# Graph attention on one core: record columns three groups ahead, and a quad's sums in front of the logits' transposes

## The chip, the core and the metric

The kernel runs on one core of a Trainium2 chip. It uses TensorE (PE), VectorE (DVE), ScalarE (ACT), GpSimd (POOL) and SyncE (SP), which run side by side, each working through its own queue of instructions in order and waiting on semaphores for the others. The metric is the device time of one execution in microseconds; the table gives the median of three runs.

## What is computed

The reference has two layers; the change touches only the first, a graph attention over 120,000 edges of 8 types between 3,750 nodes, with 4 heads of 64. The edges are sorted by destination.

```python
feat_all = jnp.einsum('ni,rhid->rnhd', inputs, conv_weights)
feat_src_e = feat_all[edge_type, edge_src]
feat_dst_e = feat_all[edge_type, edge_dst]
el = jnp.sum(feat_src_e * attn_l[edge_type], axis=-1)
er = jnp.sum(feat_dst_e * attn_r[edge_type], axis=-1)
e = jax.nn.leaky_relu(el + er, negative_slope=LEAKY_SLOPE)
m = jax.ops.segment_max(e, edge_dst, num_segments=N_NODES)
ex = jnp.exp(e - m[edge_dst])
denom = jax.ops.segment_sum(ex, edge_dst, num_segments=N_NODES)
alpha = ex / denom[edge_dst]
h = jax.ops.segment_sum(alpha[..., None] * feat_src_e, edge_dst, num_segments=N_NODES)
```

The second layer is a mixture of 8 experts, top 2, over the nodes.

## The kernel before

Five stages run one after the other: nodes (the projected features of every node and type, written to DRAM as `feats`, 260 words a row: 256 features and 4 left logits), edges, routing, experts, combination. Only `edge_stage` changes.

**Tiling.** A unit is 128 edges, a block two units. A pair is a block with one tile of 128 destination nodes. 16 pairs (32 units) make a group; there are 32 groups, the last two smaller (10 and 8 pairs). Within a group, a quad is 4 units or 2 pairs, so a full group has 8 quads. `each_period` writes a body for each group; on PE, ACT, DVE and SP group 0 stands alone, groups 1 to 24 are four rounds of a loop over six groups, and the rest is written out.

**One period, for group g.**
- SP loads the records of group g+2 (`load_meta`, 16 loads into `meta`), once the rows of group g are done (`rows_ready`).
- DVE, `meta_rows`: records to `rows`, `cat` and `reset`. PE, `meta_rows`: three transposes of `rows` into `psS` (L801). DVE, `meta_columns`: `typeT`, `idxT`, `ndlT`, then `idx_ready` (L580 to L583). Before, both are for group g+2.
- POOL, `gather_features`: after `idx_ready` one indirect DMA for each unit, 32 in all, into `gath`, which has three buffers (`GBUFS`). The gathers of a quad wait until the sums of the same quad three groups before are done.
- ACT, `one_hot`: from `ndlT` the matrix `hot` of a unit, for group g+1. PE, `turn`: its transpose; ACT, `copy`: to `hotT`. PE, `right_logits` (L825): the right logits of the edges into `psE`. DVE, `pick_right` (L589, L591) at the end of the period: `er_e` of group g+1.
- DVE, `logits` (L597, L598): after the gathers of g landed (`gath_in`), left and right logits into `e_sb`, then `e_ready`. PE: one transpose of `e_sb` into `psS` (L856), `eT_ready`. DVE, `chunk_maxima` (L604 to L607). PE: L868. DVE, `chain_maxima` (L617 to L638), `shifts`; PE and ACT between them; ACT's exponentials end with `exp_ready`.
- DVE, `scale` (L667): a quad of `gath` times its weights. PE, `total` (L840): for each of its two pairs, two accumulating products `hot` x `gath` into one of three banks of `psP`; each product is two matmul rows in the trace, so a pair is four and a quad eight. DVE, `add` (L676): the pair into its tile of `acc`, then `sum_used`.

**What sets the order.** It is written out by hand. PE's period has eight slots; slot s does `turn` of quad s and `right_logits` of quad s-1 of group g+1, and `total` of a quad: of g-1, quad s+3, in slots 0 to 4, and of g, quad s-5, in slots 5 to 7. `total` of a pair waits until the pair three before it has been added, because of the three banks. DVE's adds of quads 2 to 7 of group g-1 and of quads 0 and 1 of group g stand between its other steps: the add of quad 2 (pairs 4 and 5) directly behind `logits`, the add of quad 3 directly behind `chunk_maxima`.

## Time and profile before

| | us |
|---|---|
| median of three runs (2530.4 to 2534.8) | 2532.44 |
| the profiled run, its own time | 2529.42 |
| span of the profiled run | 2527.6 |
| edge stage, from SP's first record load to DVE's first instruction of the next stage | 283.4 to 1694.6 |
| PE, DVE, ACT, POOL busy over the span | 1860.7, 1148.7, 819.7, 1078.7 |
| mean granted clock of PE, as a share of 2.4 GHz | 0.828 |

The page gives busy time by engine and by line. A timeline row gives start, duration, engine, line, operation and output<-inputs, and in brackets the idle time before it with what ended it; "issue" is idle time that ended with nothing that the profile shows. Rows merged by the profile have a count (x8). PE's clock is granted at one of two levels, 2.4 or 1.2 GHz, which shows in the durations of the same matmuls. L597 is line 597 of the kernel before.

### The profile page before, as it was taken

The page shows a single profiled execution, that of the slowest core. Times are in us where ns is not written, and L with a number is a line of the kernel's source. Part 1 is how long each engine was busy: PE and PEld are TensorE (multiplying, and loading weights), DVE is VectorE, ACT ScalarE, POOL GpSimd, SP SyncE. Part 2 cuts the span into 40 slices and gives each one's busy share as a digit, 9 for nine tenths or more (in the row PEclk, how much of TensorE's full clock was granted, in tenths as well). Part 3 has the DMA queues.
Part 4 walks back from the last instruction along what each step waited for, and adds up shares of the span by engine and source line. Part 5 has one row for each costly group of instructions (what it writes and reads, how often), then busy time and mean ns, then how long its engine had stood idle before and what let it go on. Part 6 is the DMA issues. An engine that isn't in the chain of part 4 may idle for free. (4 is left out here: it accounts for less than half of the span.)

```text
span 2527.6 us, 38608 instructions
## 1 busy us (share of the span) xinstructions
PE 1860.7 (74%) x9120; PEld 1578.4 (62%) x9121; DVE 1148.7 (45%) x2882; ACT 819.7 (32%) x2109; POOL 1078.7 (43%) x1151
## 2 busy tenths in 40 slices
PE   6799377777777777877777878754119999999920
PEld 6688366666566665666666666544118888888820
DVE  2132136666566666666666667668411111111122
ACT  1122154444435344444444444301003223222200
POOL 1000077777676767676677777500440000000046
PEclk9899758887888788888888888875559999999965
DMA  5633244444333433343344344210135655555533
GB/s 192 249 135 153 83 117 112 111 113 107 93 106 103 109 99 106 103 111 103 102 108 106 104 113 110 77 49 17 56 138 177 205 179 201 190 193 200 184 91 113
DMA packets 127778, 317.14 MB, mean 125 GB/s; under 512 B 27207, under 2 KB 78151, under 8 KB 114020
## 3 DMA queue, kind: packets, MB, share of 16 engines
q0 software_dynamic: 53568, 148.39, 21.8%
q1 hardware_dynamic: 74020, 166.61, 19.1%
q8 instruction: 71, 1.16, 0.2%
q14 instruction: 119, 0.97, 0.1%
HBM read 251.75 MB, written 63.14 MB: 125 GB/s over the span
## 5 line engine op out<-in xcount | busy, mean ns | idle before, releaser
L552 POOL DMA_INDIRECT gath<-feats,idxT x996 | 947.1, 951 | 683.8 <-DVE ndlT L583 339.3
L840 PE MATMUL psP<-gath,hot 128*128 128x260 f32 x1992 | 627.6, 465 | 97.5 <-DVE acc L676 94.6
L840 PEld LDWEIGHTS psP<-gath,hot 128*128 128x128 f32 x1992 | 429.9, 229 | 194.3 <-DVE acc L676 108.6
L762 ACT ACTIVATE hot<-cst,ndlT 128x128 f32<-128x128 f32 x996 | 317.1, 392 | 46.7 <-DVE ndlT L583 31.5
L772 ACT COPY hotT<-psOT 128x512 f32<-128x512 f32 x249 | 144.3, 580 | 570.3 <-PE psOT L811 569.9
L667 DVE TENSOR_TENSOR gath<-gath,psA 128x1024 f32<-128x1024 f32 x249 | 301.2, 1220 | 18.0 <-ACT gath L789 11.3
L825 PEld LDWEIGHTS psE<-er,hotT 128*128 128x128 f32 x1992 | 280.7, 216 | 33.7 <-issue 31.4
L825 PE MATMUL psE<-er,hotT 128*128 x1992 | 278.5, 287 | 23.2 <-issue 23.2
L676 DVE TENSOR_TENSOR acc<-acc,psP 128x260 f32 x498 | 210.2, 422 | 116.7 <-PE psP L840 75.7
L1224 PE MATMUL psH<-xeT,w1buf 128*128 128x256 f32 x1184 | 262.8, 380 | 0.0
L1235 PE MATMUL psY<-w2buf,hT 128*128 128x256 f32 x1184 | 261.5, 379 | 0.0
L1224 PEld LDWEIGHTS psH<-xeT,w1buf 128*128 128x128 f32 x1184 | 226.0, 191 | 31.0
L401 PE MATMUL psF<-wext,xT 128*128 128x264 f32 x960 | 225.9, 394 | 23.5 <-ACT er L228 13.6
L1235 PEld LDWEIGHTS psY<-w2buf,hT 128*128 128x128 f32 x1184 | 222.2, 190 | 28.8
L1320 POOL COPY slot_col_c<-slot_i 128x2 int32 x30 | 5.8, 194 | 547.3 <-PEq L1313 546.3
L1279 DVE TENSOR_SCALAR xeT<-psX,w1buf 128x256 f32<-128x256 f32 x74 | 36.8, 539 | 412.9 <-DMA w1buf<-in_experts 400.0
L401 PEld LDWEIGHTS psF<-wext,xT 128*128 128x128 f32 x960 | 183.2, 194 | 57.1 <-ACT er L228 14.0
L1261 ACT ACTIVATE hT<-psH,w1buf 128x256 f32<-128x256 f32 x296 | 124.3, 471 | 264.3 <-PE psH L1224 264.1
L811 PE MATMUL psOT<-cst,hot 128*128 128x128 f32 x996 | 187.6, 320 | 8.3 <-issue 5.2
L811 PEld LDWEIGHTS psOT<-cst,hot 128*128 128x128 f32 x996 | 147.7, 172 | 46.1 <-issue 28.2
L765 ACT ACTIVATE hot<-hot 128x512 f32<-128x512 f32 x249 | 156.7, 629 | 7.9
L856 PE MATMUL psS<-cst,e_sb 128*128 128x128 f32 x32 | 15.2, 475 | 179.7 <-DVE e_sb L598 179.7
(190 smaller groups left out, 1220.3 us busy)
## 6 DMA issues: line engine op xcount, KB each, us to landing
w1buf<-in_experts SPq DMA_DIRECT2D x37, 1030.0 KB, 7.2
w2buf<-in_experts SPq DMA_DIRECT2D x37, 1024.0 KB, 5.4
feats<-frow SPq DMA_DIRECT2D x30, 1040.0 KB, 3.9
gath<-feats,idxT POOLq DMA_INDIRECT x996
slots_x<-acc SPq DMA_DIRECT2D x1, 9472.0 KB, 32.1
xrow<-slots_x SPq DMA_DIRECT2D x37, 256.0 KB, 6.5
slots_y<-yrow SPq DMA_DIRECT2D x37, 256.0 KB, 6.6
meta<-in_edges SPq DMA_DIRECT2D x512, 12.0 KB
```

The lines of the kernel that those rows point to most:

```text
L401: ins = pe.matmul(psF[:, n % BUFS, j, 0:W], xT[:, i % 2, k], wext[:, k, 2 * pair + j], start=k == 0, stop=k == KD - 1)
L552: pool.indirect_dma_start(gath[:, r, u], None, feats, bass.IndirectOffsetOnAxis(ap=idxT[:, q, u:u + 1], axis=0)).then_inc(gath_in[r], 16)
L667: dve.tensor_tensor(feat, feat, alpha.unsqueeze(3).to_broadcast([P, QUAD, HEADS, HD]), ALU.mult).then_inc(scaled, 1)
L676: dve.tensor_tensor(into[b % PQ], into[b % PQ], psP[:, b % BANKS, 0:FW], ALU.add).then_inc(sum_used, 1)
L762: ins = act.activation(hot[:, q, u], iota, ACT.Square, bias=ndlT[:, q, u:u + 1])
L765: act.activation(hot[:, q, j * QUAD:(j + 1) * QUAD], hot[:, q, j * QUAD:(j + 1) * QUAD], ACT.Relu, bias=1.0, scale=-1.0).then_inc(hot_read ...
L772: act.copy(hotT[:, j % 2], psOT[:]).then_inc(hotT_copied, 1)
L811: ins = pe.transpose(psOT[:, k * P:(k + 1) * P], hot[:, q, j * QUAD + k], ident)
L825: ins = pe.matmul(psE[:, u * W // 512, u * W % 512:u * W % 512 + W], hotT[:, j % 2, k * P:(k + 1) * P], tables[k // BLK], start=True, stop ...
L840: ins = pe.matmul(psP[:, b % BANKS, 0:FW], hot[:, q, u], gath[:, r, u], start=u % BLK == 0, stop=u % BLK == BLK - 1)
L1224: ins = pe.matmul(psH[:, bank(q, m // MG), (m % MG) * SLOT_TILE:(m % MG + 1) * SLOT_TILE], w1(q, k, m), xeT[:, q, k], start=k == 0, stop=k ...
L1235: ins = pe.matmul(psY[:, j, 0:D], hT[:, q, m, j * P:(j + 1) * P], w2(q, m), start=m == 0, stop=m == KH - 1)
```

## The change

Five tiles (`reset`, `cat`, `idxT`, `ndlT`, `typeT`) get three buffers, numbered by group modulo 3 like `gath`, where they had two. DVE's and PE's `meta_rows` and DVE's `meta_columns` in period g are for group g+3 in place of g+2, and three groups, not two, are done ahead of the loop. SP's loads and their waits are unchanged. In PE's period the transpose of `e_sb`, which stood in slot 0 between `turn` and `total`, stands behind slot 0. The changed kernel is two lines shorter from there on.

```diff
-        reset = t("reset", [P, 2, UNIT + 1])
-        cat = t("cat", [P, 2, 5])
-        idxT = t("idxT", [P, 2, GU], I32)
-        ndlT = t("ndlT", [P, 2, GU])
-        typeT = t("typeT", [P, 2, GU, RELS])
+        reset = t("reset", [P, GBUFS, UNIT + 1])
+        cat = t("cat", [P, GBUFS, 5])
+        idxT = t("idxT", [P, GBUFS, GU], I32)
+        ndlT = t("ndlT", [P, GBUFS, GU])
+        typeT = t("typeT", [P, GBUFS, GU, RELS])
...
-                meta_rows(0, 0)
-                meta_columns(0, 0)
-                meta_rows(1, 1)
-                meta_columns(1, 1)
+                for g in range(GBUFS):
+                    meta_rows(g, g % 2, g)
+                    meta_columns(g, g)
                 pick_right(0, 0)
...
-                    if there(g + 2):
-                        meta_rows(g + 2, q)
+                    if there(g + 3):
+                        meta_rows(g + 3, 1 - q, r)
...
-                    if there(g + 2):
-                        meta_columns(g + 2, q)
+                    if there(g + 3):
+                        meta_columns(g + 3, r)
...
-                meta_rows(0)
-                meta_rows(1)
+                for g in range(GBUFS):
+                    meta_rows(g)
                 for j in range(SLOTS_Q):
                     turn(0, 0, j)
                     right_logits(0, j - 1)
...
                 def period(g, q, r, n):
                     def slot(s):
                         turn(g + 1, 1 - q, s)
-                        if s == 0:
-                            pe.wait_ge(e_ready, g + 1)
-                            pe.transpose(psS[:, S_ET:S_ET + P], e_sb[:, 1], ident).then_inc(eT_ready, 1)
                         right_logits(g + 1, s - 1)
-                        if s == 5 and there(g + 2):
-                            meta_rows(g + 2)
+                        if s == 5 and there(g + 3):
+                            meta_rows(g + 3)
...
                     slot(0)
+                    pe.wait_ge(e_ready, g + 1)
+                    pe.transpose(psS[:, S_ET:S_ET + P], e_sb[:, 1], ident).then_inc(eT_ready, 1)
                     slot(1)
```

PE, slot 0 of a period in the loop, before; the names in brackets are the semaphores that the instruction waits for:

```order
L811 MATMUL psOT<-cst,hot 128x128 [waits hotT_copied,hot_ready]
L811 MATMUL psOT<-cst,hot 128x128 x3
L856 MATMUL psS<-cst,e_sb 128x128 [waits e_ready]
L833 REGISTER_ALU
L836 REGISTER_ALU [waits scaled]
L840 MATMUL psP<-gath,hot 128x260 [waits sum_used]
L840 MATMUL psP<-gath,hot 128x260
L836 REGISTER_ALU
L840 MATMUL psP<-gath,hot 128x260 [waits sum_used]
L840 MATMUL psP<-gath,hot 128x260
L807 REGISTER_ALU
```

The same place after:

```order
L810 MATMUL psOT<-cst,hot 128x128 [waits hotT_copied,hot_ready]
L810 MATMUL psOT<-cst,hot 128x128 x3
L832 REGISTER_ALU
L835 REGISTER_ALU [waits scaled]
L839 MATMUL psP<-gath,hot 128x260 [waits sum_used]
L839 MATMUL psP<-gath,hot 128x260
L835 REGISTER_ALU
L839 MATMUL psP<-gath,hot 128x260 [waits sum_used]
L839 MATMUL psP<-gath,hot 128x260
L863 MATMUL psS<-cst,e_sb 128x128 [waits e_ready]
L806 REGISTER_ALU
```

Both pairs' products, each with its wait for a bank, have moved in front of the wait for the logits.

DVE, ahead of the first period; what stands between the second group's columns and the first `pick_right`, before:

```order
L580 TENSOR_TENSOR typeT<-psS,cst 128x256 [waits rowsT_ready]
L582 CAST idxT<-psS 128x32 [waits v_step_edges]
L583 TENSOR_SCALAR ndlT<-psS 128x32
L589 TENSOR_TENSOR er_all<-psE,typeT 128x1024 [waits er_done]
L591 TENSOR_REDUCE er_e<-er_all 128x128 [waits v_step_edges]
```

After:

```order
L583 TENSOR_SCALAR ndlT<-psS 128x32
L565 SCALAR_TENSOR_TENSOR rows<-meta 128x128 [waits meta_in0]
L566 CAST rows<-meta 128x128
L567 TENSOR_SCALAR rows<-meta,tile_off 128x128
L570 TENSOR_SCALAR cat<-rows,tile_of 128x2 [waits rows_ready]
L572 COPY cat<-rows 128x1
L573 MEMSET reset 128x2
L574 TENSOR_TENSOR reset<-rows 128x127
L575 TENSOR_SCALAR reset<-reset 128x127 [waits v_step_edges]
L580 TENSOR_TENSOR typeT<-psS,cst 128x256 [waits rowsT_ready]
L582 CAST idxT<-psS 128x32 [waits v_step_edges]
L583 TENSOR_SCALAR ndlT<-psS 128x32
```

Eleven instructions of the third group, the first with a wait for its records, stand in front of `pick_right`. On PE the three transposes of its rows stand in front of the first `turn`.

## Rows read from the trace of the kernel before

**Rows 1.** Page, costliest groups (busy, mean ns | idle before); then L597 by source.

```profile
L552 POOL DMA_INDIRECT gath<-feats,idxT x996 | 947.1, 951 | 683.8 <-DVE ndlT L583 339.3
...
L597 DVE TENSOR_TENSOR e_sb<-gath,er_e x32: 291/292/344, 352.3 to 1666.2; 128x128 f32<-128x128 f32 x32
```

**Rows 2.** Waits over the span: us in total, times, longest.

```profile
POOL gath L552 <- DVE ndlT L583: 339.3, 16, 300.7
POOL gath L552 <- issue: 285.1, 933, 0.6
...
PE psS L856 <- DVE e_sb L598: 179.7, 32, 7.1
...
DVE lv L617 <- PE psS L868: 57.1, 32, 4.3
```

**Rows 3.** Timeline of PE, parts of two periods: start, us, engine, instructions.

```profile
1011.63 1.12 PE L811 MATMUL psOT<-cst,hot 128*128 128x128 f32 x4
1012.54 1.76 PE L825 MATMUL psE<-er,hotT 128*128 x8
...
1035.19 0.64 PE L811 MATMUL psOT<-cst,hot 128*128 128x128 f32 x4
1041.55 0.48 PE L856 MATMUL psS<-cst,e_sb 128*128 128x128 f32 x1 [5.72 <-DVE e_sb L598]
1041.82 3.67 PE L840 MATMUL psP<-gath,hot 128*128 128x260 f32 x8
1045.29 0.82 PE L811 MATMUL psOT<-cst,hot 128*128 128x128 f32 x4
1045.95 0.98 PE L825 MATMUL psE<-er,hotT 128*128 x8
1046.76 2.00 PE L840 MATMUL psP<-gath,hot 128*128 128x260 f32 x8
1048.69 0.43 PE L868 MATMUL psS<-spread,cst 128*4 128x160 f32 x2
```

**Rows 4.** Timeline of DVE, the same period and the next logits.

```profile
1040.72 0.29 DVE L597 TENSOR_TENSOR e_sb<-gath,er_e 128x128 f32<-128x128 f32 x1 [2.85 <-issue]
...
1041.41 0.98 DVE L676 TENSOR_TENSOR acc<-acc,psP 128x260 f32 x2
1042.43 1.22 DVE L667 TENSOR_TENSOR gath<-gath,psA 128x1024 f32<-128x1024 f32 x1
1043.57 0.41 DVE L604 TENSOR_TENSOR_SCAN seg<-reset,psS 128x128 f32<-128x128 f32 x1
...
1044.92 0.42 DVE L676 TENSOR_TENSOR acc<-acc,psP 128x260 f32 x1
...
1049.16 0.18 DVE L617 COPY lv<-psS 4x32 f32<-4x32 f32 x1 [1.84 <-PE psS L868]
...
1082.73 0.29 DVE L597 TENSOR_TENSOR e_sb<-gath,er_e 128x128 f32<-128x128 f32 x1 [2.86 <-issue]
```

**Rows 5.** Timeline of POOL: the first gather of each of two groups.

```profile
1028.45 0.95 POOL L552 DMA_INDIRECT gath<-feats,idxT  x1 [2.16 <-PE psP L840]
...
1072.15 0.95 POOL L552 DMA_INDIRECT gath<-feats,idxT  x1 [3.72 <-DVE ndlT L583]
```

**Rows 6.** Timelines of DVE and SP at the start of the edge stage.

```profile
304.76 0.29 DVE L565 SCALAR_TENSOR_TENSOR rows<-meta 128x128 f32<-128x128 int32 x1 [22.55 <-DMA meta<-in_edges]
...
326.22 0.29 DVE L565 SCALAR_TENSOR_TENSOR rows<-meta 128x128 f32<-128x128 int32 x1 [19.09 <-DMA meta<-in_edges]
...
389.95 0.29 DVE L597 TENSOR_TENSOR e_sb<-gath,er_e 128x128 f32<-128x128 f32 x1 [4.20 <-DMA gath<-feats,idxT]
...
283.41 106.21 SPq L530 DMA_DIRECT2D meta<-in_edges  x80
```

**Rows 7.** Timeline of DVE: a group's rows in a period, up to the next add.

```profile
1021.92 0.29 DVE L565 SCALAR_TENSOR_TENSOR rows<-meta 128x128 f32<-128x128 int32 x1 [1.69 <-issue]
...
1023.48 0.42 DVE L676 TENSOR_TENSOR acc<-acc,psP 128x260 f32 x1
```

More of the change, by code:

```diff
@@ L568, in meta_rows, with meta_columns, pick_right @@
                     dve.wait_ge(rows_ready, g + 1)
-                    dve.tensor_scalar(cat[:, q, 2:4], rows[:, 1, 0:UNIT:UNIT - 1], 64.0, sb["tile_of"][:, bass.ds(g, 1)],
+                    dve.tensor_scalar(cat[:, r, 2:4], rows[:, 1, 0:UNIT:UNIT - 1], 64.0, sb["tile_of"][:, bass.ds(g, 1)],
                                       ALU.mult, ALU.add)
-                    dve.tensor_copy(cat[:, q, 4:5], rows[:, 1, 0:1])
-                    dve.memset(reset[:, q, 0:UNIT + 1:UNIT], 0.0)
-                    step(dve.tensor_tensor(reset[:, q, 1:UNIT], rows[:, 1, 1:UNIT], rows[:, 1, 0:UNIT - 1], ALU.not_equal))
-                    dve.tensor_scalar(reset[:, q, 1:UNIT], reset[:, q, 1:UNIT], -BIG, None, ALU.mult)
-                def meta_columns(g, q):
+                    dve.tensor_copy(cat[:, r, 4:5], rows[:, 1, 0:1])
+                    dve.memset(reset[:, r, 0:UNIT + 1:UNIT], 0.0)
+                    step(dve.tensor_tensor(reset[:, r, 1:UNIT], rows[:, 1, 1:UNIT], rows[:, 1, 0:UNIT - 1], ALU.not_equal))
+                    dve.tensor_scalar(reset[:, r, 1:UNIT], reset[:, r, 1:UNIT], -BIG, None, ALU.mult)
+                def meta_columns(g, r):
                     dve.wait_ge(rowsT_ready, g + 1)
-                    step(dve.tensor_tensor(typeT[:, q], psS[:, 2 * P:3 * P:HEADS].unsqueeze(2).to_broadcast([P, GU, RELS]),
+                    step(dve.tensor_tensor(typeT[:, r], psS[:, 2 * P:3 * P:HEADS].unsqueeze(2).to_broadcast([P, GU, RELS]),
                                            iota8.unsqueeze(1).to_broadcast([P, GU, RELS]), ALU.is_equal))
-                    dve.tensor_copy(idxT[:, q], psS[:, 0:P:HEADS])
-                    dve.tensor_scalar(ndlT[:, q], psS[:, P:2 * P:HEADS], -1.0, None, ALU.mult).then_inc(idx_ready, 1)
-                def pick_right(g, q):
+                    dve.tensor_copy(idxT[:, r], psS[:, 0:P:HEADS])
+                    dve.tensor_scalar(ndlT[:, r], psS[:, P:2 * P:HEADS], -1.0, None, ALU.mult).then_inc(idx_ready, 1)
+                def pick_right(g, r):
                     dve.wait_ge(er_done, quads_before(g) + quads(g))
@@ L638, in chain_maxima, with shifts @@
                     step(dve.tensor_copy(r_last[:, 0:1], r_last[:, used:used + 1]))
-                def shifts(g, q):
-                    fwd, bwd = reset[:, q, 0:UNIT], reset[:, q, UNIT:0:-1]
+                def shifts(g, r):
+                    fwd, bwd = reset[:, r, 0:UNIT], reset[:, r, UNIT:0:-1]
                     dve.wait_ge(yzT_ready, g + 1)
@@ L706, in period @@
                     scale(before, rb, 4)
-                    chunk_maxima(g, q)
+                    chunk_maxima(g, r)
                     add(before, 3, sums3)
@@ L717, in period @@
                     sums5, sums6 = load_tiles(before, 5), load_tiles(before, 6)
-                    shifts(g, q)
+                    shifts(g, r)
                     add(before, 5, sums5)
@@ L740, in period @@
                     if there(g + 1):
-                        pick_right(g + 1, 1 - q)
+                        pick_right(g + 1, (r + 1) % GBUFS)
                     assert isinstance(g, int) or step.n == STEPS, step.n
@@ L751, in _, with one_hot @@
             def _(act):
-                def one_hot(g, q, j):
+                def one_hot(g, q, r, j):
                     if j >= quads(g):
@@ L761, in one_hot @@
                         u = j * QUAD + k
-                        ins = act.activation(hot[:, q, u], iota, ACT.Square, bias=ndlT[:, q, u:u + 1])
+                        ins = act.activation(hot[:, q, u], iota, ACT.Square, bias=ndlT[:, r, u:u + 1])
                     ins.then_inc(squared, 1)
@@ L772, in copy, with both @@
                     act.copy(hotT[:, j % 2], psOT[:]).then_inc(hotT_copied, 1)
-                def both(g, q, js):
+                def both(g, q, r, js):
                     for j in js:
-                        one_hot(g, q, j)
+                        one_hot(g, q, r, j)
                         if j:
                             copy(g, j - 1)
-                both(0, 0, range(SLOTS_Q))
+                both(0, 0, 0, range(SLOTS_Q))
                 copy(0, SLOTS_Q - 1)
                 def period(g, q, r, n):
-                    both(g + 1, 1 - q, range(5))
+                    both(g + 1, 1 - q, (r + 1) % GBUFS, range(5))
                     act.wait_ge(dnT_ready, g + 1)
@@ L790, in period @@
                                    ACT.Exp).then_inc(exp_ready, 1)
-                    both(g + 1, 1 - q, range(5, SLOTS_Q))
+                    both(g + 1, 1 - q, (r + 1) % GBUFS, range(5, SLOTS_Q))
                     copy(g + 1, SLOTS_Q - 1)
```

14 lines of the change are left out of this document (7 added, 7 removed).

## The prediction

> **What bounds the kernel now.** I began with the page's groups and the waits, then laid the time rows of PE and DVE in one period of the edge stage side by side, then read the start of that stage. The edge stage repeats one period per group of edges; the 32 logits instructions at L597 run from 352.3 to 1666.2 [rows 1], so a period takes 1313.9 / 31 = 42.4 us. No engine fills it. GpSimd comes closest: 996 gathers of 951 ns, with 285.1 us of issue time between them, are 1.24 us each, 39.6 us for the 32 of a full group, and it has idle time besides [rows 1, 2]. The period is a ring of hand-overs between PE and DVE. Its widest hole on PE is the wait for the logits, 179.7 us in 32 times, 5.6 us each. DVE in turn waits for PE's L868, 57.1 us in 32 times, 1.8 us each [rows 2]. So in the stretch from the logits to L617, PE's queue ends last and DVE has 1.8 us to spare.
>
> In one period: PE ends the one-hot transposes at 1035.83, is idle until 1041.55, transposes the logits, runs quad 3's eight matmuls (3.67 us), then transposes, right logits, quad 4's matmuls and L868 at 1048.69 [rows 3]. DVE makes the logits at 1040.72, adds pairs 4 and 5, scales quad 4, is ready for the logits' maxima at 1043.57 with no wait, adds pair 6 at 1044.92, and waits 1.84 us for L868 before L617 at 1049.16 [rows 4].
>
> **Part 1, quad 3's sums in front of the logits' transposes.** The quad is pairs 6 and 7, four matmuls each. psP has three banks: pair 6 needs pair 3 added, done in the previous period; pair 7 needs pair 4 added, and that add stands on DVE behind the logits. So only half the quad can move into the 5.7 us hole, and the other half now stands between the logits and their transposes.
>
> Pair 6 starts at 1035.8 at the fast rate, half of quad 4's 2.00 us = 1.0, and is out of the way by 1036.9. Pair 7 starts after pair 4's add, which is half of the 0.98 us from 1041.41, so at 1041.95, and takes half of 3.67 us = 1.84: until 1043.8. The transpose (0.48) then ends near 1044.3. Two consequences:
> - DVE's maxima start 1044.3 instead of 1043.57, 0.7 us later. That fits into the 1.84 us that DVE waits for L868 today: 1.1 us of it are left [rows 4].
> - PE begins slot 1 near 1044.05 instead of 1045.29, 1.24 us earlier. Not all of this arrives. The matmuls after the hole run at half rate until about 1045.9: eight in 3.67 us against 2.00 [rows 3]. If this stretch ends at the same time as before, slot 1 now lies in it: its transposes cost up to 1.12 instead of 0.82, and part of its right logits goes at 1.76 instead of 0.98, together 0.3 to 0.6 lost. Pair 9 needs pair 6's add, now ending at 1046.0; PE reaches pair 9 near 1047, so that doesn't bind.
>
> So L868 and L617 come 0.6 us earlier. After L617 all is a chain (some twenty small DVE steps, then PE waiting for DVE's adds), which only shifts. Bounds: 0.2 if slot 1 is slow throughout (1.24 - 0.30 - 0.78), and 1.1, the DVE wait that is left. I take **0.6**, the reading in the middle of the slow stretch. The 31 periods with a quad in front give 31 x 0.6 = **-18.6 us** (-6 to -34).
>
> **Part 2, columns three groups ahead.** In the loop this moves no work off PE or DVE: the same eleven DVE instructions and three transposes stand in the same slots, for group g+3. It releases GpSimd: of its waits for L583, 339.3 - 300.7 = 38.6 us, those inside the loop, go [rows 2]. Nobody waits for that. Gathers of the group that starts at 1028.45 end before 1072.15 minus the 3.72 us wait, at 1068.4, and their logits come at 1082.73, 14 us later [rows 4, 5]. So **0 us** in the loop. If this cover were gone, the price would be what the gathers are late; none shows. SP's loads keep their wait (rows of g done, group g+2 loaded), which now comes a period sooner, and the loads stay two periods ahead of use.
>
> It costs something at the start. Before the first one-hot transpose PE now also has to pass the third group's rows transposes, and those wait for its records. SP issues record loads back to back, 80 in 106.21 us, 1.33 each, 21.2 us for a group's 16; the first group's landed for DVE at 304.76, the second's at 326.22 [rows 6], so the third's at 347.5. DVE, PE (its turns, its right logits), ACT's copies behind PE's turns and then pick_right and the logits all come 21.3 us later. What comes back is small: the second logits had waited 4.20 us for gathers, where 2.86 us is the usual gap [rows 4, 6]; with everything later the gathers are there, so 1.3 us return. **+20.0 us**, bounds 18 and 21.5. Nothing hides it: the period that follows has no slack of that size on any engine, since the ring has none.
>
> One period at the end has no rows and columns any more. Up to the next add they take DVE from 1021.92 to 1023.48, 1.56 us [rows 7], on DVE's path between two adds: **-1.5 us** (0 to -2.5).
>
> **Sum.** +20.0 - 18.6 - 1.5 = -0.1 us. The profiled run took 2529.42 us, so 2529.3; the median of the runs shown is 3.0 us above it. The forecast is **2532 us**, no measurable change, where 0.2% or 5 us is about what a measurement can tell. By the bounds: best 18 - 34 - 2.5 = -18.5, worst 21.5 - 6 = +15.5.
>
> **Rivals.**
> - *The slow stretch swallows the gain* (2542 us). PE comes back from the hole at half rate, and with its matmuls earlier more of slot 1 is slow. For: eight matmuls take 3.67 us after the hole in this period, and right logits elsewhere take 1.76. Against: the slow stretch has to reach past 1046. At 0.2 to 0.3 us per period it gives -8, so +20 - 8 - 1.5 = +10.5. This is the case that ends slower, and it decides from a gain under 0.45 us per period, where the net is above +5.
> - *DVE's chain becomes the bound* (2572 us). If the maxima come so late that L617 no longer waits for PE, each period grows by about 0.7 instead of shrinking: 31 x 0.7 + 18.5 = +40. It needs the transposed logits more than 1.8 us late; worked out they are 0.7. Unlikely.
> - *PE's clock stays up* (2517 us). Four matmuls cut the hole from 5.7 to about 5.1 us, and the return after it may then be at the fast rate. Pair 7 takes 1.0, the transposed logits are there for DVE near 1043.5 with no delay, and L617 can come 1.1 us earlier: 31 x 1.1 = 34, net 20 - 34 - 1.5 = -15.5. Against it: 5.1 us is still nearly the whole hole. The Trainium skill, "TensorE: Matmul & The Clock Gate", Part 1, says of the clock: "the default state is throttled, and activity releases the throttle". By that rule filling the hole is right in kind; the slow 3.67 us after it agree with the rule, and whether four matmuls suffice no row of before shows.
> - *The gathers did bind* (2464 us). If some of GpSimd's lateness is hidden in the 2.86 us before each logits, the period could fall to GpSimd's own 39.6: 31 x 2.8 = 87, net 20 - 87 - 1.5 = -68. The 14 us of margin speak against it.
> - *The third group's records cost nothing* (2512 us), if the added DVE and PE work did not stand in the queues in front of the first turns; the order of instructions says that it does.
>
> **How the numbers follow.** Forecast 0.41 (gain 0.45 to 0.8 per period, own range 2526 to 2538); slow stretch 0.22; clock up 0.22; DVE bound 0.07; gathers 0.04; free start 0.04. Range: 2510 to 2550. It takes in the forecast, the slow stretch and the clock case with the bounds of the sum around 2532 (+15.5 gives 2548, -18.5 gives 2514) and a little beyond, and leaves out DVE bound, gathers and the edges of the rest, under 0.2. Faster by over 0.2%: clock 0.22, gathers 0.04, free start 0.04 and 0.07 of the forecast, 0.37. Slower: 0.22 + 0.07 and 0.03 of the forecast, 0.32. The rest, 0.31, is no change.
>
> **What the new profile would show.** The first logits near 373.8 instead of 352.3, the second near 410 without a wait for gathers; a third wait of DVE for records, about 19 us. In the loop: four psP matmuls right behind the one-hot transposes, then an idle time of about 5 us that ends with DVE's add (L676) and not with the logits; L604 waiting some 0.7 us for PE; L617's wait down from 1.8 to about 0.5; 41.8 us per period; GpSimd's waits for ndlT gone. Wrong would be: first logits before 365, a period above 42.4, eight matmuls behind the transposes instead of four in front, or L617 not waiting at all.

## The result and the profile after

| | before | after |
|---|---|---|
| median of four runs each, on the same chip, us | 2532.28 | 2583.15 |
| lowest and highest, us | 2530.4 to 2534.8 | 2582.65 to 2585.49 |
| profiled run, us (span) | 2529.42 (2527.6) | 2585.49 (2583.7) |
| mean granted clock of PE | 0.828 | 0.814 |
| first, second, last logits, us | 352.3, 389.95, 1666.15 | 371.40, 407.30, 1721.19 |

After/before is **1.021, 95% interval 1.0196 to 1.0224**: 50.9 us slower. The forecast was 2532 us, no measurable change, with a range up to 2550. The time lies 33 us above that range.

The difference of the two profiled runs, 56.1 us, splits at the logits (L597): +17.4 up to the second ones, +37.7 in the 30 periods from there to the last (1313.9 us against 1276.2, which is 1.26 a period), +0.3 to the end of the edge stage, +0.8 behind it. So the start cost about what was forecast, and the loop, which should have given 18.6 us, took 37.7.

The page after: its first lines, and the two groups that answer to [rows 1] and to the quads' sums.

```profile
span 2583.7 us, 38612 instructions
...
PE 1917.8 (74%) x9120; PEld 1618.0 (63%) x9121; DVE 1153.9 (45%) x2882; ACT 819.2 (32%) x2109; POOL 1079.0 (42%) x1151
...
L552 POOL DMA_INDIRECT gath<-feats,idxT x996 | 947.7, 952 | 698.0 <-DVE ndlT L583 316.6
...
L839 PE MATMUL psP<-gath,hot 128*128 128x260 f32 x1992 | 662.0, 483 | 249.7 <-DVE acc L676 246.7
```

The same 9120 matmuls keep PE busy for 1917.8 us where it was 1860.7: 57.1 us more for the same work, while PE's idle time stays what it was (2583.7 - 1917.8 = 665.9 us against 666.9). DVE, ACT and POOL are busy as before. That is the first sign of where the time went: not a new wait, but slower matmuls.

The waits of after (us in total, times, longest), beside [rows 2]:

```profile
POOL gath L552 <- DVE ndlT L583: 316.6, 19, 298.5
...
PE psP L839 <- DVE acc L676: 246.7, 87, 6.6
...
POOL gath L552 <- PE psP L839: 110.6, 94, 4.4
...
DVE lv L617 <- PE psS L866: 22.2, 32, 3.1
```

PE's wait for the logits, 179.7 us before, is gone; in its place stands the wait for DVE's add. DVE's wait at L617 fell from 57.1 to 22.2 us, as the change means it to. GpSimd waits more for free buffers (94 times, 110.6 us) and less for indices: besides the longest wait, 316.6 - 298.5 = 18.1 us are left of the 38.6 that the prediction expected to go.

PE in one period of after, which answers to [rows 3] (start, us, engine, line, work, idle before):

```profile
1074.35 1.04 PE L839 MATMUL psP<-gath,hot 128*128 128x260 f32 x4
1080.81 2.10 PE L839 MATMUL psP<-gath,hot 128*128 128x260 f32 x4 [5.42 <-DVE acc L676]
1082.71 0.42 PE L863 MATMUL psS<-cst,e_sb 128*128 128x128 f32 x1
1082.92 1.06 PE L810 MATMUL psOT<-cst,hot 128*128 128x128 f32 x4
1083.77 1.14 PE L824 MATMUL psE<-er,hotT 128*128 x8
1084.74 2.00 PE L839 MATMUL psP<-gath,hot 128*128 128x260 f32 x8
...
1091.70 2.10 PE L839 MATMUL psP<-gath,hot 128*128 128x260 f32 x4 [2.23 <-DVE acc L676]
...
1094.77 1.11 PE L810 MATMUL psOT<-cst,hot 128*128 128x128 f32 x4
1095.68 1.75 PE L824 MATMUL psE<-er,hotT 128*128 x8
1097.25 3.81 PE L839 MATMUL psP<-gath,hot 128*128 128x260 f32 x8
1100.85 0.42 PE L875 MATMUL psS<-cst,dn 128*128 128x128 f32 x1
```

And PE of before in the second half of that stretch, which the rows ahead of the prediction did not reach:

```profile
1053.76 1.14 PE L840 MATMUL psP<-gath,hot 128*128 128x260 f32 x4 [2.27 <-DVE acc L676]
...
1055.42 0.66 PE L811 MATMUL psOT<-cst,hot 128*128 128x128 f32 x4
1055.91 0.98 PE L825 MATMUL psE<-er,hotT 128*128 x8
1056.72 1.12 PE L840 MATMUL psP<-gath,hot 128*128 128x260 f32 x4
1059.46 2.10 PE L840 MATMUL psP<-gath,hot 128*128 128x260 f32 x4 [1.61 <-DVE acc L676]
1061.36 0.42 PE L877 MATMUL psS<-cst,dn 128*128 128x128 f32 x1
```

Read them as pairs. The hole ahead of the period's first sums is 5.42 us against 5.72, and the matmuls behind it are at the lower rate in both (four in 2.10 us after, eight in 3.67 before). The second hole has the same length, 2.23 against 2.27 us, and ends with the same add. Before, the four matmuls behind it take 1.14 us; after, they take 2.10, and everything behind them up to L875 is slow too: one-hot transposes 1.11 against 0.66, right logits 1.75 against 0.98, eight sums 3.81. From the first of these sums to the `dn` transpose it is 9.15 us after and 7.60 before.

The two periods stand for the rest in the main point. Over the 22 periods from the third logits to the 25th, the four matmuls behind the second hole (pair 11) take 1.14 to 1.15 us in every period of before and 2.10 in every period of after, behind holes of 2.38 and 2.48 us on average. Beyond that pair the rows of before show a better period than most: the next one (pair 12), 1.12 us here, takes over 1.6 us in 15 of the 22 periods of before and in all 22 of after.

The loop's windows (us, then busy time with instructions of PE, PEld, DVE, ACT and POOL, then PE's granted clock, DMA share, GB/s), from the third to the 25th logits; before, then after:

```profile
433.10:1385.76 952.66, 729.99 (x3762) 604.50 (x3762) 618.34 (x1562) 424.89 (x1122) 675.62 (x712) 0.83 0.40 105
```

```profile
451.30:1437.99 986.69, 779.25 (x3762) 641.20 (x3762) 623.13 (x1563) 424.59 (x1122) 691.02 (x726) 0.80 0.39 104
```

With the two levels at 1 and 0.5 of full speed, a mean clock c means a share 2 x (1 - c) at the lower one: 0.34 of 43.3 us before, 0.40 of 44.9 after. Summed from the clock's records it is 15.1 us a period before and 18.3 after. For the same 3762 matmuls PE is busy (779.25 - 729.99) / 22 = 2.24 us longer in each period.

The full period of before is 43.3 us, and not the prediction's 42.4: that is a mean over all 31 periods, with the shorter ones at the end in it.

Means over those 22 periods, in us after L597's start, show where in the period the time is won and lost:

| | before | after | difference |
|---|---|---|---|
| DVE's maxima start (L604) | 2.73 | 3.35 | +0.62 |
| DVE L617 | 8.27 | 7.52 | -0.75 |
| DVE L649 (end of the small steps) | 18.11 | 17.40 | -0.71 |
| PE's `dn` transpose (L877, after L875) | 20.74 | 21.47 | +0.73 |
| DVE's rows (L565) | 24.87 | 25.58 | +0.70 |
| DVE `pick_right` (L589) | 37.41 | 38.94 | +1.53 |
| next logits | 43.30 | 44.85 | +1.55 |

The gain is there, of the size forecast, and it holds as far as L649. Then 1.4 us are lost around the second hole and another 0.8 in the last slots, where slow stretches stand as well. The gain of 0.75 and the 1.55 that the period is longer make 2.30, about the 2.24 by which PE's busy time grew. One slow stretch of the last slots:

```profile
1107.91 3.68 PE L839 MATMUL psP<-gath,hot 128*128 128x260 f32 x8 [0.56 <-DVE acc L676]
```

Before, the same eight took 1.99 us, at 1068.38.

**Theory.** The moved matmuls change how PE's work and idle time lie in the period, and more of the work then runs at the lower clock; the hand-overs themselves are right. **Rivals.** (a) The three-deep columns cost the time, through GpSimd or the DMAs. (b) The logits' transpose now waits behind pair 7, and that delay costs it. (c) The gathers collide with the sums that now start earlier.

### The profile page after: what moved, and what is told of

Same layout as the page of the kernel before. It is cut to its first block and busy times, and to the rows that moved or that the text cites. A ratio compares the mean times of both kernels' runs of the same rounds, so it can differ in the third digit from the quotient of the medians.

```text
span 2583.7 us, 38612 instructions
## 1 busy us (share of the span) xinstructions
PE 1917.8 (74%) x9120; PEld 1618.0 (63%) x9121; DVE 1153.9 (45%) x2882; ACT 819.2 (32%) x2109; POOL 1079.0 (42%) x1151
## 5 line engine op out<-in xcount | busy, mean ns | idle before, releaser
L552 POOL DMA_INDIRECT gath<-feats,idxT x996 | 947.7, 952 | 698.0 <-DVE ndlT L583 316.6
L839 PE MATMUL psP<-gath,hot 128*128 128x260 f32 x1992 | 662.0, 483 | 249.7 <-DVE acc L676 246.7
L839 PEld LDWEIGHTS psP<-gath,hot 128*128 128x128 f32 x1992 | 439.5, 235 | 354.2 <-DVE acc L676 264.2
L824 PEld LDWEIGHTS psE<-er,hotT 128*128 128x128 f32 x1992 | 294.0, 225 | 38.8 <-issue 36.5
L824 PE MATMUL psE<-er,hotT 128*128 x1992 | 290.1, 294 | 28.2 <-issue 28.2
L667 DVE TENSOR_TENSOR gath<-gath,psA 128x1024 f32<-128x1024 f32 x249 | 301.2, 1219 | 17.0 <-ACT gath L788 10.3
L810 PE MATMUL psOT<-cst,hot 128*128 128x128 f32 x996 | 195.2, 330 | 7.3 <-ACT hot L764 6.0
L1094 POOL DMA_INDIRECT slots_x<-xn,slot_col x60 | 57.6, 959 | 219.1 <-DVE xn L1078 199.3
```

What stands on the lines that cost most here:

```text
L552: pool.indirect_dma_start(gath[:, r, u], None, feats, bass.IndirectOffsetOnAxis(ap=idxT[:, r, u:u + 1], axis=0)).then_inc(gath_in[r], 16)
L667: dve.tensor_tensor(feat, feat, alpha.unsqueeze(3).to_broadcast([P, QUAD, HEADS, HD]), ALU.mult).then_inc(scaled, 1)
L810: ins = pe.transpose(psOT[:, k * P:(k + 1) * P], hot[:, q, j * QUAD + k], ident)
L824: ins = pe.matmul(psE[:, u * W // 512, u * W % 512:u * W % 512 + W], hotT[:, j % 2, k * P:(k + 1) * P], tables[k // BLK], start=True, stop ...
L839: ins = pe.matmul(psP[:, b % BANKS, 0:FW], hot[:, q, u], gath[:, r, u], start=u % BLK == 0, stop=u % BLK == BLK - 1)
```

## Experiments

### On a chip of another kind

The first runs fell on chips on which the kernel before itself takes 3600 to 3700 us. In what follows, the first kind of chip is the one on which it takes about 2530 us.

**e1_order_alone**: `before` with PE's order changed and nothing else.

```diff
-                        if s == 0:
-                            pe.wait_ge(e_ready, g + 1)
-                            pe.transpose(psS[:, S_ET:S_ET + P], e_sb[:, 1], ident).then_inc(eT_ready, 1)
...
                     slot(0)
+                    pe.wait_ge(e_ready, g + 1)
+                    pe.transpose(psS[:, S_ET:S_ET + P], e_sb[:, 1], ident).then_inc(eT_ready, 1)
```

> The kernel before with the logits' transposes behind quad 3's sums and nothing else changed. Both theories (the clock theory: PE spends more of each period at its lower clock; the order theory: a wait of PE or DVE grew) expect the loss in the loop here: 30 periods x 1.3 us = 38 us, so about 2568 us, a period near 43.8 us, the first logits at 352. If the columns made three groups in advance had a share in the loop's loss, this run is well below 2568.

**e2_ahead_alone**: `after` with the transpose put back into slot 0, so only the columns are three groups ahead (the same lines the other way round).

> The kernel after with the logits' transposes back in slot 0, between the one-hot transposes and quad 3's sums: columns three groups ahead alone. Expected by both: the start only, +17 us (in the changed kernel the second logits came 17.4 us later), no change in the loop, 1 us less at the end: about 2549 us. A rival, that the earlier gathers disturb the loop, expects a period above 42.5 us and more than 2555 us.

**e3_between_pairs**: `before` with the transpose between pair 6 and pair 7, so that it need not wait for pair 7.

```diff
+                        if between and b == PQ * j:
+                            between()
...
+                    def between():
+                        pe.wait_ge(e_ready, g + 1)
+                        pe.transpose(psS[:, S_ET:S_ET + P], e_sb[:, 1], ident).then_inc(eT_ready, 1)
```

> The kernel before with pair 6 (the first half of quad 3) in front of the logits' transposes and pair 7 behind them. DVE's maxima then wait for nothing new. Order theory (PE's wait for the add of pair 4 in front of the logits' transposes costs the time): the loss is gone and L617 comes over 1 us earlier than before: 2500 to 2515 us. Clock theory (taking work out of the time behind the hole lets the lower clock reach further into the period): L617 comes earlier too, but the matmuls of pair 11 and of slots 2 and 3 run at the lower rate, and the total is 2530 to 2570 us.

**e4_order_filled**: e1, with the hole between pair 6 and pair 7 filled by eight matmuls whose result nobody reads (every group but the first).

```diff
+                    def between():
+                        for _ in range(0 if isinstance(g, int) and g == 0 else 8):
+                            pe.matmul(psS[:, 0:2 * P], ident, cst[:, 0:2 * P], start=True, stop=True)
```

> The order of e1 with 8 extra 128x256 matmuls (some 3.6 us at the higher clock) in the hole between pair 6 and pair 7, written into a part of psS that nobody needs at that time; they compute nothing that is used. Clock theory: the stretch at the lower clock behind the hole goes or gets shorter, and the period falls well below e1's 43.8, to 41 to 42 us: 2490 to 2520 us in spite of the extra work. Order theory: the period stays at 43.8 or above: 2565 us or more.

**e5_before_filled**: `before` with ten such matmuls in front of the wait for the logits.

```diff
                         if s == 0:
+                            for _ in range(0 if isinstance(g, int) and g == 0 else 10):
+                                pe.matmul(psS[:, 0:2 * P], ident, cst[:, 0:2 * P], start=True, stop=True)
                             pe.wait_ge(e_ready, g + 1)
```

> The kernel before with 10 extra 128x256 matmuls (some 4.4 us at the higher clock) in the hole of 5.7 us between the one-hot transposes and the logits' transposes, written into a part of psS that nobody needs at that time; they compute nothing that is used. Clock theory: the eight matmuls of quad 3 behind the logits' transposes take 2.0 us, not 3.7, the period gets shorter by 1 us or more, 2485 to 2510 us. If the lower clock costs nothing on the ring of waits, 2532 us or slower by what the filler delays.

**e6_after_again**: the changed kernel as it is, to see what kind of chip this is.

> The changed kernel itself, once more, beside the kernel before. In the earlier runs of this study the kernel before took 3612 to 3686 us instead of 2532, with 40 us in every period in which DVE (L589) and ACT (L772) wait while GpSimd works through a group's gathers. If that state holds here too, the changed kernel, whose gathers start earlier, takes about 2950 us like the run with the columns three groups ahead alone; if it doesn't, 2583 us.

| | us | before on that chip | ratio, 95% interval |
|---|---|---|---|
| e1_order_alone | 3703.01 | 3686.29 | 1.0042 (1.0023 to 1.0061) |
| e2_ahead_alone | 2938.55 | 3686.29 | 0.7973 (0.7929 to 0.8017) |
| e3_between_pairs | 3707.29 | 3686.29 | 1.0062 (1.0041 to 1.0083) |
| e4_order_filled | 3706.96 | 3686.29 | 1.0058 (1.0034 to 1.0082) |
| e5_before_filled | 3622.36 | 3612.11 | 1.0014 (0.9980 to 1.0048) |
| e6_after_again | 2985.05 (one run) | 3703.32 | 0.81 |

None of e1 to e5 came near its expected time, and these runs answer another question than the one asked; e6 took 2985 us, where 2950 was expected if the chip was of this kind. The waits of e1:

```profile
PE psP L840 <- DVE acc L676: 1252.5, 89, 45.2
ACT hotT L772 <- remote: 1114.9, 41, 39.3
DVE er_all L589 <- remote: 1083.8, 28, 41.8
```

and one period of it, from the timelines of POOL, PE, DVE and ACT ("remote": the profile shows nothing that released the wait):

```profile
1508.72 0.94 POOL L552 DMA_INDIRECT gath<-feats,idxT  x1 [45.55 <-PE psP L840]
...
1547.46 0.95 POOL L552 DMA_INDIRECT gath<-feats,idxT  x1 [0.30 <-issue]
```

```profile
1516.65 1.07 PE L825 MATMUL psE<-er,hotT 128*128 x8 [1.90 <-issue]
...
1560.32 2.10 PE L840 MATMUL psP<-gath,hot 128*128 128x260 f32 x4 [39.67 <-DVE acc L676]
```

```profile
1553.97 1.23 DVE L589 TENSOR_TENSOR er_all<-psE,typeT 128x1024 f32<-128x1024 f32 x1 [40.48 <-remote]
```

```profile
1554.03 0.58 ACT L772 COPY hotT<-psOT 128x512 f32<-128x512 f32 x1 [33.85 <-remote]
```

DVE waits for right logits whose matmuls PE has on record at 1516.65, and goes on only at 1553.97, after the last of the 32 gathers of the group. Then PE starts, then GpSimd: the gathers and the rest of the period stand one behind the other, 82 us in place of 43. The gathers themselves take 0.95 us each as elsewhere. With the columns three groups ahead, GpSimd has its indices early and its gathers overlap more of the period (in e2 DVE's wait is no longer among the largest, ACT's is 404.4 us where e1 has 1114.9), and the kernel takes 0.80 of the time.

The filler of e4 shows more. Its sixteen rows wait for nothing, and while the gathers run PE still starts them one at a time:

```profile
1529.09 0.59 PE L858 MATMUL psS<-cst 128*128 128x256 f32 x1 [2.27 <-issue]
1531.90 0.59 PE L858 MATMUL psS<-cst 128*128 128x256 f32 x1 [2.21 <-issue]
```

From one row's start to the next it is 2.1 us in the median there, and 0.22 in f4, the same kernel on a chip of the first kind. So on these chips PE too falls behind during the gathers, in instructions that no semaphore holds, and the long waits of DVE and ACT need not be waits for a semaphore alone. What slows them is not shown by any record, and stays open.

It also means that the fillers of e4 and e5 don't keep PE busy here, and the matmuls behind the first hole stay slow (pair 7 of e5 takes 1.83 us on average). The second hole differs as well: e1's pair 11 takes over 1.6 us in 7 of 22 periods, where f1 below has 22 of 22. e1, e3 and e4 differ by less than their intervals. So the theory had to be tested without the gathers, or on a chip like the first.

### Without the gathers

The n-kernels leave out the gathers of groups 3 to 31 and the waits for them; the buffers keep the first groups' rows, so their times stand for the ring of PE, DVE and ACT alone. This time the chip was of the first kind, `before` at 2530.66 us.

```diff
-                each_period(pool, gather_features, GBUFS, GROUPS - 3)
+                for g in range(GBUFS):
+                    gather_features(g, g % 2, g, 0)
...
-                    dve.wait_ge(gath_in[r], landed(g, r, n))
+                    if isinstance(g, int) and g < GBUFS or not isinstance(g, int):
+                        dve.wait_ge(gath_in[r], landed(r, r, 0))
```

**n1_base** is `before` with this edit alone; **n2_order**, **n3_between** and **n4_order_filled** add the edits of e1, e3 and e4.

> The kernel before without the gathers of groups 3 to 31: the first three groups are gathered, and later groups use what their buffer still holds, so the features and logits are not the reference's. Everything on PE, DVE, ACT and SP stays. In this study the kernel before has taken 3612 to 3703 us with 40 us in each period in which DVE and ACT wait while GpSimd issues gathers; if the gathers are what makes them wait, this run has a period of 42.5 us as in the trace of before, and about 2535 us or somewhat less. If the wait has another source, 80 us a period stay.

> The same without gathers, with the logits' transposes behind quad 3's sums. Both theories of the loop's loss (PE's lower clock reaching further, or a longer wait in the ring) expect it here as well: a period 1.3 us longer than n1_base, 43.8 us, some 40 us in all. If it is the gathers' timing that makes the order slow, the period is that of n1_base or shorter.

> Without gathers, pair 6 in front of the logits' transposes and pair 7 behind them. Theory of the wait: L617 comes over 1 us earlier than in n1_base and so does all behind it: 41 to 41.5 us a period. Clock theory: L617 comes earlier, and the matmuls of pair 11 and of slots 2 and 3 run at the lower rate, so the period is 42.5 to 44 us.

> Without gathers, the order of n2_order with 8 extra 128x256 matmuls between pair 6 and pair 7, which compute nothing that is used. Clock theory: less time at the lower clock than n2_order and a period of 41 to 42.5 us. Theory of the wait: 43.8 us or more.

| | us | ratio to before, 95% interval | period, us | at the lower clock, us a period |
|---|---|---|---|---|
| n1_base | 2509.85 | 0.9923 (0.9895 to 0.9952) | 42.52 | 14.0 |
| n2_order | 2557.82 | 1.0113 (1.0042 to 1.0185) | 44.73 | 20.0 |
| n3_between | 2561.96 | 1.0107 (1.0059 to 1.0154) | 44.40 | 18.9 |
| n4_order_filled | 2511.24 | 0.9931 (0.9915 to 0.9946) | 43.12 | 13.0 |

With no gather in the loop the order costs 48 us (n2 against n1, two runs each, n2's 15 us apart): rival (c) falls, and with it GpSimd's part in (a). n3 starts the maxima at 2.74 us, as n1 does, and is as slow as n2: rival (b) falls. Matmuls that compute nothing take 46.6 us away again (n4 against n2).

Not all of it came as expected. Both theories had L617 earlier in n3, and it isn't: 8.11 us after the logits in n1, 8.17 in n2, 8.33 in n3. Here the slow stretch behind the first hole reaches the next quad's sums in some periods (pair 8 takes over 1.6 us in 10 of 22 periods of n3, in 5 of n2 and in none of n1), which is the prediction's rival *the slow stretch swallows the gain*. The loss itself lies behind L649 again. n2's and n3's periods, 44.73 and 44.40, are longer than forecast (43.8; 42.5 to 44), and so is n4's, 43.12 (41 to 42.5).

### The parts and the filler, on a chip of the first kind

The kernels of e1, e2, e4 and e5 again, together on one chip where `before` takes 2532.73 us (eight runs, 2529.6 to 2537.9).

> The kernel before with the logits' transposes behind quad 3's sums, with gathers, on a chip where the kernel before takes 2530 us. Clock theory, as in n2_order against n1_base (+48 us): 2565 to 2580 us. If the columns ahead carried part of the loop's loss: below 2555 us.

> Columns three groups ahead alone, the logits' transposes in slot 0 as before. The start costs 17 to 20 us, the end gives 1.5 us, the loop nothing: 2546 to 2550 us. If earlier gathers disturb the loop, above 2555 us; if they help it, below 2540 us.

> f1_order_alone with 8 extra 128x256 matmuls, which compute nothing that is used, in the hole between pair 6 and pair 7. Clock theory, as n4_order_filled against n2_order (-47 us): 2520 to 2535 us. If the gathers or another wait hold the period: as f1_order_alone.

> The kernel before with 10 extra 128x256 matmuls in the hole in front of the logits' transposes. Clock theory: quad 3's eight matmuls take 2.0 us where they took 3.7, the period drops by 1 us or more, 2485 to 2510 us. If the lower clock behind the hole is hidden by other waits: 2530 us.

| | us | ratio to before, 95% interval | second, last logits | period | at the lower clock |
|---|---|---|---|---|---|
| before (first profile) | 2532.73 | 1 | 389.95, 1666.2 | 43.30 | 15.1 |
| f1_order_alone | 2572.19 | 1.0149 (1.0132 to 1.0166) | 388.3, 1708.5 | 44.88 | 19.8 |
| f2_ahead_alone | 2542.99 | 1.0038 (1.0024 to 1.0053) | 407.4, 1673.1 | 42.96 | 15.2 |
| f4_order_filled | 2522.40 | 0.9952 (0.9935 to 0.9968) | 389.0, 1661.2 | 43.17 | 12.6 |
| f5_before_filled | 2515.54 | 0.9938 (0.9915 to 0.9961) | 388.4, 1643.2 | 42.53 | 11.8 |

The last three columns are of the profiled run, which for f2 and f5 was the fastest, 5.6 and 8.0 us under the median. f1 and f4 came as the clock theory had it. f2 lies 3 us below its forecast, and above the 2540 of the rival. f5 missed: 2485 to 2510 us and a period shorter by 1 us or more were expected, and it gave 2515.5 and 0.77.

The two parts add up: 2572.19 - 2532.73 = 39.5 for the order and 10.3 for the columns make 49.7, and the whole change took 50.9. **The order is the loss.** Its period has the marks of `after` to within 0.03 us (L617 at 7.54, L565 at 25.55, L589 at 38.93), with columns two groups ahead, so rival (a) falls entirely. Two more marks agree: f1's PE is busy 2.37 us longer in each of the 22 periods, against 0.73 gained at L617 and 1.58 lost by the period, 2.31; and its pair 11 is slow in all of them. The time at the lower clock is a poorer measure: after has 18.3 us a period and f1 19.8, with the same period to 0.03 us.

f4 is the direct test: f1 with 16 more matmul rows in each period and not a wait less. PE of f1 and then of f4 at the same place:

```profile
1063.91 2.10 PE L840 MATMUL psP<-gath,hot 128*128 128x260 f32 x4 [5.19 <-DVE acc L676]
...
1068.15 2.00 PE L840 MATMUL psP<-gath,hot 128*128 128x260 f32 x8
...
1075.21 2.10 PE L840 MATMUL psP<-gath,hot 128*128 128x260 f32 x4 [2.33 <-DVE acc L676]
```

```profile
1032.22 3.62 PE L858 MATMUL psS<-cst 128*128 128x256 f32 x16
1037.60 1.14 PE L842 MATMUL psP<-gath,hot 128*128 128x260 f32 x4 [1.76 <-DVE acc L676]
...
1048.01 2.10 PE L842 MATMUL psP<-gath,hot 128*128 128x260 f32 x4 [2.84 <-DVE acc L676]
```

The hole shrinks from 5.19 to 1.76 us of idle time, its end is the same add, and pair 7 takes 1.14 us instead of 2.10. L617 comes at 6.86 us instead of 7.54, the time at the lower clock falls from 19.8 to 12.6 us a period, and the kernel is 49.8 us faster. The Trainium skill, "TensorE: Matmul & The Clock Gate", Part 1, says that "the default state is throttled, and activity releases the throttle"; by that rule useless matmuls are activity too, and pair 7's rows agree. Pair 11's don't change: 2.10 us in both.

The same filler in `before` (f5), at the place of [rows 3]:

```profile
1061.73 4.48 PE L856 MATMUL psS<-cst 128*128 128x256 f32 x20
1067.47 0.33 PE L858 MATMUL psS<-cst,e_sb 128*128 128x128 f32 x1 [1.25 <-DVE e_sb L598]
1067.64 1.93 PE L840 MATMUL psP<-gath,hot 128*128 128x260 f32 x8
...
1078.37 2.10 PE L840 MATMUL psP<-gath,hot 128*128 128x260 f32 x4 [3.00 <-DVE acc L676]
```

Quad 3's eight matmuls take 1.93 us where [rows 3] has 3.67, and DVE then hardly waits for PE at L617 (9 times, 6.2 us in all, of 57.1):

```profile
1073.43 0.18 DVE L617 COPY lv<-psS 4x32 f32<-4x32 f32 x1 [0.21 <-issue]
```

This is the fastest version found that computes the result, 17.2 us under `before`. f4 against f5 shows what the order is worth with the first hole filled: nothing, L617 at 6.86 against 6.66 us, and 6.9 us in all the wrong way, with runs that overlap (2520.2 to 2526.3, 2507.6 to 2523.7). The clock is not out of it: in both, the second hole (2.84 and 3.00 us) still has half-rate sums behind it.

The same 22 periods, for all the kernels: in how many of them four matmuls take over 1.6 us (at the higher clock they take 1.0 to 1.2, at the lower one 1.9 to 2.1), and the mean time from L617 to the `dn` transpose.

| | pair 7, behind the first hole | pair 11, behind the second | L617 to `dn`, us |
|---|---|---|---|
| before | 20 | 0 | 12.47 |
| after | 22 | 22 | 13.95 |
| f1_order_alone | 22 | 22 | 13.90 |
| f2_ahead_alone | 15 | 0 | 12.42 |
| f4_order_filled | 2 | 21 | 13.70 |
| f5_before_filled | 0 | 17 | 13.60 |
| n1_base | 18 | 0 | 12.30 |
| n2_order | 22 | 18 | 13.52 |
| n3_between | 22 | 11 | 13.11 |
| n4_order_filled | 4 | 13 | 13.37 |

Between f1 and before, with pair 11 slow in one and fast in the other, the order costs 1.43 us in this stretch; between f4 and f5, slow in both, 0.10. That ties the loss at the second hole to the rate of PE's matmuls and not to the order of the waits. The table also says what the filler does: it brings back the rate behind the first hole alone. It does not repair the second hole, and in f5 it makes the matmuls there slow that were fast in before. L617 comes 1.61 us earlier in f5, and 1.13 of them are lost again by the `dn` transpose, which is where f5's forecast failed.

### Both holes filled

**f6_before_both** and **f9_before_both** are one kernel: f5, and four more matmuls in the second hole. **f7_between_both** is the order of e3 with both holes filled, **f8_between_filled** that order with the first hole alone.

```diff
+                    def second():
+                        if not there(g + 1) or isinstance(g, int) and (g == 0 or g + 1 >= GROUPS - 2):
+                            return
+                        pe.wait_ge(hotT_copied, quads_before(g + 1) + 3)
+                        for _ in range(4):
+                            pe.matmul(psOT[:, 0:2 * P], ident, cst[:, 0:2 * P], start=True, stop=True)
```

> f5_before_filled (10 extra matmuls in the hole in front of the logits' transposes) and 4 more, some 1.8 us at the higher clock, in the 2.3 us that PE waits between pair 10 and pair 11. Clock theory: the slow stretch behind that hole (slots 2 and 3) goes too, another 0.5 to 1 us a period: 2480 to 2505 us. If only the first hole sets the clock: 2515 us or, where the extra matmuls are late, somewhat more.

> Pair 6 in front of the logits' transposes, then 8 extra matmuls, the transposes, pair 7, and 4 extra matmuls between pair 10 and pair 11. With the clock held up, the order itself can show its gain: L617 over 1 us earlier than in f6_before_both, 2470 to 2500 us. If the order gains nothing even at the higher clock: the time of f6_before_both.

> f7_between_both without the 4 extra matmuls between pair 10 and pair 11. Clock theory with both holes counting: 15 to 30 us slower than f7_between_both. If only the first hole counts: the same as f7_between_both. Against f4_order_filled (2522 us) it shows what the wait of the logits' transposes for pair 7 costs with a filled hole: 0.6 us a period of DVE's, some 10 to 20 us.

> The kernel of f6_before_both once more, on whatever chip it meets. Where the kernel before takes 2530 us: clock theory with both holes counting 2480 to 2505 us; if only the first hole counts, 2515 us, the time of f5_before_filled. Where the kernel before takes 3600 us, it tells nothing new.

| | us | before on that chip | ratio, 95% interval |
|---|---|---|---|
| f6_before_both | 3535.56 | 3607.90 | 0.9797 (0.9767 to 0.9827) |
| f7_between_both | 3554.42 | 3607.90 | 0.9865 (0.9812 to 0.9919) |
| f8_between_filled | 3665.96 | 3607.90 | 1.0139 (1.0102 to 1.0177) |
| f9_before_both | 3530.79 | 3607.54 | 0.9779 (0.9744 to 0.9814) |

All four met chips of the other kind. There the second filler is worth 2 to 3% (f6 and f9, where the first alone gave 1.0014 in e5; f7 is 111.5 us faster than f8, where 15 to 30 were forecast). The order gains nothing with both fillers either: f7 takes 18.9 us more than f6.

The second hole is about the same there as on the first kind, 2.26 us in f8, and f7 shrinks it to 0.54. Pair 11 is slow in 18 of 22 periods of f8 and in none of f7, f6 likewise. So four matmuls do keep the rate up behind this hole. But that is not where the time is won: in f7 L565 comes 24.88 us after the logits against 25.18 in f8, and L589 70.45 against 75.88, so 5.1 us a period are won behind L565, where the gathers run. The edit also makes PE wait for ACT's third copy ahead of the four matmuls, and what part of this is the wait's was not told apart. What the second filler would bring on a chip of the first kind stays open.

## Why the prediction was wrong

**The start** (+20.0 forecast, bounds 18 and 21.5): the mechanism was right, the size 0.6 us below the lower bound. The third wait for records is 19.01 us, forecast 19; the records are there at 345.33, forecast 347.5; the first logits come 19.1 us later (forecast 21.3) and the second 17.4, since no wait for gathers is left there:

```profile
345.33 0.29 DVE L565 SCALAR_TENSOR_TENSOR rows<-meta 128x128 f32<-128x128 int32 x1 [19.01 <-DMA meta<-in_edges]
371.40 0.29 DVE L597 TENSOR_TENSOR e_sb<-gath,er_e 128x128 f32<-128x128 f32 x1
...
407.30 0.31 DVE L597 TENSOR_TENSOR e_sb<-gath,er_e 128x128 f32<-128x128 f32 x1 [3.12 <-issue]
```

**Columns ahead in the loop** (0 forecast): some 7 us too pessimistic, by the medians: f2 loses 10.3 us in all, 17.4 of them at the start. In its profiled run, 5.6 us faster than the median, the 30 periods from the second logits on take 1265.7 us against 1276.2. About half of it is in one period, the seventh after the start, 50.0 us in `before` and 44.5 in f2; the rest is a few tenths in many. Why it is shorter in f2 no run settles. The end term (-1.5) can't be told from these variations.

**The hole and L617** (0.6 us a period forecast, bounds 0.2 and 1.1): right, 0.75. The shape was right too: four sums behind the one-hot transposes, 5.42 us of idle time ending with the add (forecast about 5), L604 0.62 us later (forecast 0.7).

**The step that failed** is the sentence behind it, "After L617 all is a chain ... which only shifts". It took the durations of PE's matmuls beyond the hole as given. They are not: with the sums moved forward, the matmuls behind the *next* hole, about as long as before, ran at half rate up to the `dn` transpose, in all of the 22 periods where before has none. The chain from L649 on costs 2.3 us more a period (from -0.71 to +1.55), and that turned -18.6 into +37.7, with part 2's gain already in it (f1, without that gain, loses 44.1 us from the second logits to the last).

The rival *the slow stretch swallows the gain* had the mechanism and was mis-sized: it let the stretch behind the first hole reach a little further, worth 0.3 us, and never asked about the other holes. What it needed was the clock over the whole period: 15.1 us at the lower level, spread over several stretches. That number was to be had from the trace of before. It said that PE spent a third of the period at the lower clock, and the prediction looked at one stretch of it. With the order alone it grew by 4.7 us; at half rate 4.7 us do the work of 2.35, which covers the 1.58 that f1's period is longer and the 0.73 that it had gained. With the whole change it grew by only 3.2 us, for the same loss: there PE's busy time gives the sum (2.24 us), and this count doesn't.

*PE's clock stays up* was right in kind as well. The four rows of pair 6 were too few for it, sixteen more brought it (f4), and it gave 12.6 us a period at the lower clock in place of 19.8. *DVE's chain becomes the bound* fell: L617 still waits, 22.2 us in all. *The gathers did bind* fell on this chip (n1 gains 21 us with no gathers in the loop, where the rival had 87); on the other kind of chip the columns ahead do gain, 0.80 of the time in e2.

What stays open: by what the clock falls behind a hole of 2.2 us in one order and not in the other. The runs show that it does, in 1.14 against 2.10 us for the same four matmuls, and not why. The length of the hole doesn't sort them: 2.38 us on average in before and 2.29 in n1, with no slow period, 2.48 in after, 2.42 in f1 and 2.27 in n2, slow in 22, 22 and 18.

## What to carry to other kernels

Before moving matmuls on a PE with holes, list every hole of the period with the rate of the matmuls behind it, and add up the time at the lower clock: a move priced only at the hole that it fills can be lost at the next one. Then compare the rates again after the change, over many periods and at every hole: a filler in one hole made the matmuls behind another one slow. If PE comes back slow behind a hole of several us that can't be closed with work, try matmuls that nobody reads in it before any reordering; here ten of them gave 17 us, about what the reordering was meant to give, and the reordering with such a filler gave nothing more. That holds for the chips where the kernel before takes 2530 us; on the others the same ten gave nothing (e5). And time the two halves of a change apart: here +39.5 and +10.3.

## What the runs showed of the chip that was not expected

- Moving four of some 170 matmul rows of a period across one idle wait and half a quad ahead of one transpose raised the time at the lower clock from 15.1 to 19.8 us a period, and the kernel's time by 1.5% (f1). The matmuls that became slow stand 11 us further on, behind another wait of about 2.4 us, which did not change.
- Matmuls that compute nothing made the kernel 49.8 us (f4 against f1), 46.6 us (n4 against n2) and 17.2 us (f5 against before) faster.
- A filler in one hole restores the rate behind it (pair 7 slow in 0 of 22 periods of f5, 20 before) and can take it away behind the next (pair 11 slow in 17, none before).
- Indirect gathers cost this kernel little on a chip of the first kind: leaving out 900 of 996 gave 21 us (n1).
- There are chips on which the kernel before takes 3600 to 3700 us. While GpSimd issues a group's 32 gathers, DVE and ACT sit up to 42 and 39 us in waits that no record releases, and PE starts matmuls that wait for nothing 2.1 us apart in place of 0.22 (e4 against f4). The gathers' early indices are worth 20% there (e2), and cost 0.4% on the other kind (f2): which version is the better one depends on the chip.
